# Two graph layers in one kernel: the attention product moved next to z, h turned by eight DMA transposes, x products among the additions, two buffers for h

## The reference

```python
# layer 1, for every sample
q, k = wq @ x, wk @ x                                  # 512 each
att = softmax(leaky_relu(q[None, :] + k[:, None]))     # 512 x 512
x = layernorm(x + relu(adj @ (x @ att.T) + bm))        # h in the kernel
# layer 2, on h (256 rows of 512)
A_l = relu(cosine similarity of the rows of h @ W_lang.T), diagonal 0
A_g = exp(-squared distances of the rows of h @ W_grav.T / (2 sigma^2)), diagonal 0
K   = w * rownorm(A_l * adj) + (1 - w) * rownorm(A_g * adj)
x   = layernorm(h + K @ (h @ W_V.T) @ W_O.T)
```

## Time and profile before

| | us |
|---|---|
| median of 3 runs | 1072.63 (1071.83 to 1072.81) |
| the profiled execution | 1072.26 |
| its span, first to last instruction | 1070.3 |
| TensorE busy | 1043.2 |
| VectorE busy | 877.3 |
| ScalarE busy | 634.3 |
| GpSimd busy | 325.0 |

### The profile page before, as it was taken

One profiled execution on the slowest core, in us unless ns is written; L12 is line 12 of the kernel. 1 busy time (PEld: TensorE's weight loads), 2 busy tenths in 40 slices (PEclk: granted clock), 3 DMA queues, 4 the chain that ended last, 5 costly groups with the idle time before them and its releaser, 6 DMA issues.

```text
span 1070.3 us, 20032 instructions
## 1 busy us (share of the span) xinstructions
PE 1043.2 (97%) x7429; PEld 723.4 (68%) x7429; DVE 877.3 (82%) x2442; ACT 634.3 (59%) x1203; POOL 325.0 (30%) x280
## 2 busy tenths in 40 slices
PE   7989999999999999999999999999999999999995
PEld 5466767677676766767676676767667676766662
DVE  4767787888889888888988888898888889888767
ACT  2656566485665748566574856657485664748431
POOL 0333315243341524324151432405143240514100
PEclk9999999999999999999999999999999999999998
DMA  7020011030301103030020303002030300202011
GB/s 274 21 77 4 1 64 57 1 119 1 119 1 52 68 1 119 1 119 1 34 87 1 118 2 119 1 26 94 2 118 2 116 5 16 104 2 79 1 40 40
DMA packets 22833, 56.33 MB, mean 53 GB/s; under 512 B 1744, under 2 KB 2256, under 8 KB 20688
## 3 DMA queue, kind: packets, MB, share of 16 engines
q1 hardware_dynamic: 22736, 55.06, 14.1%
HBM read 21.50 MB, written 16.78 MB: 36 GB/s over the span
## 4 chain that ended last, share of the span: by engine, by line
PE 92%; issue 3%; DVE 3%; ACT 1%; POOL 1%; DMA 0%; POOLq 0%; DVEq 0%
PE bank L223 26%; PE bank L224 26%; PE bank L225 26%; PE bank L345 3%; PE bank L428 2%; PE bank L479 2%; PE bank L230 2%; PE bank L259 2%; PE bank L419 1%; PE bank L276 0%; DVE h L1057 0%; POOL y L1129 0%; DMA agg_t<-in_wl 0%; DVE y_stat L1022 0%; ACT y L627 0%
## 5 line engine op out<-in xcount | busy, mean ns | idle before, releaser
L1112 POOL TENSOR_TENSOR att_lo<-att,att_hi 128x512 f16<-128x512 f32 x128 | 157.9, 1245 | 219.8 <-ACT att_hi L532 219.8
L862 DVE SCALAR_TENSOR_TENSOR att<-a_row,u_col,vb 128x512 f32<-128x512 f32 x128 | 126.7, 1010 | 30.3 <-POOL att_lo L1112 30.3
L573 ACT ACTIVATE z_hi<-bank 128x512 f16<-128x512 f32 x128 | 75.7, 591 | 117.1 <-PE bank L225 116.4
L223 PE MATMUL bank<-xw_hi,att_hi 128*128 128x257 f16 x512 | 140.5, 274 | 1.2 <-DVE wvo_lo L746 1.0
L225 PE MATMUL bank<-ht_hi,z_lo 128*128 128x256 f16 x512 | 139.6, 273 | 0.0
L223 PE MATMUL bank<-ht_hi,z_hi 128*128 128x256 f16 x512 | 139.6, 273 | 0.0
L224 PE MATMUL bank<-ht_lo,z_hi 128*128 128x256 f16 x512 | 139.6, 273 | 0.0
L225 PE MATMUL bank<-xw_hi,att_lo 128*128 128x257 f16 x512 | 139.5, 272 | 0.0
L224 PE MATMUL bank<-xw_lo,att_hi 128*128 128x257 f16 x512 | 139.1, 272 | 0.0
L869 DVE TENSOR_TENSOR z_lo<-bank,z_hi 128x512 f16<-128x512 f32 x128 | 87.6, 690 | 39.8 <-ACT z_hi L573 37.7
L634 ACT ACTIVATE xw_hi<-bank 128x256 f16<-128x256 f32 x128 | 49.1, 385 | 107.4 <-PE bank L225 107.4
(11 more groups left out here) (173 smaller groups left out, 2703.4 us busy)
## 6 DMA issues: line engine op xcount, KB each, us to landing
x_in<-in_x SPq DMA_DIRECT2D x16, 1024.0 KB, 5.5
x_res<-x_in SPq DMA_DIRECT2D x16, 1024.0 KB, 5.3
out_y<-o SPq DMA_DIRECT2D x32, 512.0 KB, 3.3
agg_t<-in_wl SPq DMA_DIRECT2D x4, 256.0 KB, 3.6
y<-in_wg SPq DMA_DIRECT2D x1, 1024.0 KB, 9.3
o<-in_wv SPq DMA_DIRECT2D x1, 1024.0 KB, 11.5
h<-in_woT SPq DMA_DIRECT2D x1, 1024.0 KB, 13.7
att<-in_adjT SPq DMA_DIRECT2D x1, 256.0 KB, 4.1
```

Source lines behind the costliest of these rows:

```text
L223: pe.matmul(dst, ah, bh, start=(i == 0 and first), stop=False, skip_group_check=skip)
L573: act.activation(z_hi[:, g, :], bank[g % 4][:], ACT.Copy).then_inc(s["z_hi_done"], 1)
L862: dve.scalar_tensor_tensor(out=att[:, g % 2, :], in0=a_row[:, j, :], scalar=u_col[:, j, n:n + 1], in1=vb[:, g % 2, :], op0=ALU.mult, op1=A ...
L1112: pool.tensor_tensor(att_lo[:, n[0], n[1], :], att[:, g % 2, :], att_hi[:, n[0], n[1], :], ALU.subtract).then_inc(s["att_lo_done"], 1)
```

## The change

The arithmetic of every tile stays. What changes is the place of the work, who does some of it, and where the tiles lie.

- h, ht_hi and ht_lo get two buffers, by the pair's parity. To make room v_hi, v_lo become parts of z_hi, z_lo, kt becomes a part of t, diag_junk a part of vb.
- h of pair q is split before it is turned: h_hi by ScalarE, h_lo by GpSimd, in fp16, in the space of att_hi, att_lo. Eight DMA transposes of 128 x 512 on SP's queue then write ht_hi and ht_lo. Only pair 0 is still turned by TensorE.
- The attention products stand right behind the z products, the turn of agg behind them, ahead of t. On ScalarE and VectorE the attention tiles are interleaved with z_hi and z_lo from the start of the step.
- `k_rows`, `t_rows` and the exps for the attention of pair r are at the end of step p, not in step p + 1. For pair 1 they stand in step 0 on TensorE, and at the end of step -1's list on VectorE and ScalarE.
- The x products, in banks 0 to 2, stand between the t products and the additions. The v products follow the additions.
- The scaling of a_l by s_l is done by ScalarE (`k_scale`).
- o_stats, o_norm and the store of pair p - 1 come in step p as before, but all the o_stats of the last pair follow all its residuals.

Lines of the diff, cut to the core:

```diff
-        h = sb("h", [2 * OC, N])
-        ht_hi, ht_lo = sb("ht_hi", [DC, 2 * O], F16), sb("ht_lo", [DC, 2 * O], F16)
+        h2 = sb("h", [2, 2 * OC, N])
+        ht2_hi, ht2_lo = sb("ht_hi", [2, DC, 2 * O], F16), sb("ht_lo", [2, DC, 2 * O], F16)
...
+        v_hi, v_lo = z_hi[:, 0:2 * OC, :], z_lo[:, 0:2 * OC, :]
+        diag_junk = vb[:].rearrange("p a (b n) -> p (a b) n", n=P)
...
+        kt_hi, kt_lo = t_hi[:, 0:2], t_lo[:, 0:2]
+        h_hi, h_lo = att_hi[:, 0], att_lo[:, 0]
...
+            def turn_h(pair):
+
+                hi, lo = ht_of(pair)
+                for k in range(4):
+                    cols = slice(k * P, (k + 1) * P)
+                    sp.wait_ge(s["h_hi_done"], 4 * (pair - 1) + k + 1)
+                    sp.dma_start_transpose(hi[:, :, cols], h_hi[:, k, :]).then_inc(s["ht_hi_landed"], 16)
+                    sp.wait_ge(s["h_lo_done"], 4 * (pair - 1) + k + 1)
+                    sp.dma_start_transpose(lo[:, :, cols], h_lo[:, k, :]).then_inc(s["ht_lo_landed"], 16)
...
+                if p >= 1:
+                    store(p - 1)
+                if p >= 0 and l0:
+                    turn_h(q)
```

TensorE's new step (p from 0 on; the products themselves are as before):

```diff
+                if p > 0:
+                    pe.wait_ge(s["ht_hi_landed"], 64 * p)
+                    pe.wait_ge(s["ht_lo_landed"], 64 * p)
+                for g in range(8):
...
+                    if p > 0 and l0 and g == 2:
+                        pe.wait_ge(s["t_done"], 2 * q + 2)
+                    if p > 0 and g < 2:
+                        pe.wait_ge(s["o_done"], 4 * p - 3 + g)
+                    if g >= 4:
+                        pe.wait_ge(s["z_lo_done"], 8 * p + g - 3)
...
+                    if at(p, 0) and g == 1:
+                        k_rows(1)
+
+                if l0:
+                    for k in range(8):
+                        pe.wait_ge(s["att_lo_done"], 8 * q + 4 * (k // NC) + 4)
+                        if k < 4:
+                            pe.wait_ge(s["z_lo_done"], 8 * p + 5 + k)
+                        att_product(q, k)
...
+                if l0:
+                    turn_agg(q)
+                for k in range(4):
+                    t_product(k)
+                if new:
+                    for k in range(3):
                         wx_product(k)
...
+                add_transposed(0)
+                add_transposed(1)
+                norm_rows()
+                if new:
+                    for k in range(3, 6):
                         wx_product(k)
+                else:
+                    v_product(0)
+                add_transposed(2)
+                if new:
+                    wx_product(6)
+                    wx_product(7)
+                add_transposed(3)
+                if new:
+                    v_product(0)
+                v_product(1)
+                v_product(2)
+                turn_k(0)
+                turn_k(1)
+                if new:
+                    pe.wait_ge(s["v_lo_done"], 4 * p + 1)
+                    k_rows(r)
+                v_product(3)
+                for k in range(4):
+                    o_product(k)
```

ScalarE's new step:

```diff
                 if l0:
+                    vb_tile(q, 0)
+                    vb_tile(q, 1)
+                    z_hi_tile(0)
+                    for g in range(8):
+                        att_hi_tile(q, g)
+                        if g < 6:
+                            vb_tile(q, g + 2)
+                        for i, after in enumerate((0, 2, 3, 4, 5, 6)):
+                            if g == after:
+                                z_hi_tile(i + 1)
+                    z_hi_tile(7)
                     for k in range(8):
...
+                        agg_tile(q, k)
+                        if new and k in (1, 3):
+                            x_hi_tile(k // 2)
+                    for k in range(4):
+                        relu_tile(q, k)
...
+                t_hi_tile(0)
+                t_hi_tile(1)
                 if l0:
...
+                    h_hi_tile(0)
+                    h_hi_tile(1)
+                t_hi_tile(2)
                 if l0:
...
+                    h_hi_tile(2)
+                    h_hi_tile(3)
+                t_hi_tile(3)
+                if new:
+                    for k in range(3):
+                        xw_hi_tile(p, k)
```

It goes on with xw_hi 3 to 5, the exps of A_g with xw_hi 6 and 7 between them, v_hi 0, the scaling of a_l, v_hi 1 and 2, kt_hi, v_hi 3, the exps of the attention rows of r. VectorE's new step:

```diff
                 if l0:
...
+                    for g in range(8):
+                        att_tile(q, g)
+                        for i, after in enumerate((0, 1, 3, 4, 5, 6, 7)):
+                            if g == after:
+                                z_lo_tile(i)
+                    z_lo_tile(7)
+                    den(q, 0)
+                    o_stats()
+                    den(q, 1)
+                    den(q, 2)
+                    den(q, 3)
+                    o_norms()
                     for k in range(4, 8):
...
+                        den(q, k)
+                    for k in (0, 2):
+                        y_add_tile(q, k)
+                        y_stat_tile(q, k)
+                    y_stat_tile(q, 1)
+                    y_stat_tile(q, 3)
+                    y_mean(q)
+                    sq_tile(0)
+                    t_lo_tile(0)
+                    sq_tile(1)
+                    sq_bound()
+                    h_tile(q, 0)
+                    h_tile(q, 1)
+                    t_lo_tile(1)
+                    neg_g_tile(0)
+                    h_tile(q, 2)
+                    h_tile(q, 3)
...
+                neg_g_tile(1)
+                t_lo_tile(2)
...
+                if new:
+                    for k in range(3):
+                        xw_lo_tile(p, k)
+                t_lo_tile(3)
+                masked_rows()
+                if new:
+                    for k in range(3, 6):
+                        xw_lo_tile(p, k)
```

More of the change, by code:

```diff
@@ new lines, in k_rows, with att_product @@
+            def k_rows(q):
+                pe.wait_ge(s["q_part_done"], q + 1)
+                for j in range(2):
+                    last = spread(bank[6][:, j * P:(j + 1) * P], q_part[:, j:j + 1])
+                last.then_inc(s["q_mm"], 1)
+                for j, b in enumerate(k_bank(q)):
+                    for n in range(NC):
+                        last = spread(bank[b][:, n * P:(n + 1) * P], qk[:, j * NC + n, 1:2])
+                    last.then_inc(s["k_mm"], 1)
+            def att_product(q, k):
+                j, m = k // NC, slice((k % NC) * P, (k % NC + 1) * P)
+                if k >= 4:
+                    pe.wait_ge(s["agg_done"], 8 * q + k - 3)
+                product(bank[k % 4][:, 0:O + 1], [(att_hi[:, j, n, m], att_lo[:, j, n, m],
+                                                   xw_hi[:, j, n, 0:O + 1], xw_lo[:, j, n, 0:O + 1])
+                                                  for n in range(NC)]).then_inc(s["ot_mm"], 1)
@@ new lines, in turn_agg, with wx_matmuls @@
+            def turn_agg(q):
+                for k in range(4):
+                    if k < 3:
+                        pe.wait_ge(s["agg_done"], 8 * q + (5, 6, 8)[k])
+                    j, c = k // 2, slice((k % 2) * P, (k % 2 + 1) * P)
+                    for m in range(NC):
+                        last = pe.transpose(bank[k][:, m * P:(m + 1) * P], agg_t[:, j, m, c], ident[:])
+                    last.then_inc(s["to_mm"], 1)
+            def wx_matmuls(p, k):
+                j, n = k // NC, slice((k % NC) * P, (k % NC + 1) * P)
+                product(wx_bank(p, k)[:, 0:OW],
+                        [(x_hi[:, j, c, n], x_lo[:, j, c, n], wm_hi[:, c, :], wm_lo[:, c, :])
+                         for c in range(CC)]).then_inc(s["wx_mm"], 1)
@@ L644, in step, with k_scale @@
-                if new and not at(p, -1):
-                    for k in range(4, 8):
-                        xw_hi_tile(k)
+                    act.activation(v_hi[:, k, :], bank[v_bank[k]][:], ACT.Copy).then_inc(s["v_hi_done"], 1)
+                def k_scale():
+                    act.wait_ge(s["sl_done"], p + 1)
+                    for k in range(4):
+                        act.activation(a_l[:, k // 2, k % 2, :], a_l[:, k // 2, k % 2, :], ACT.Copy,
+                                       scale=s_l[:, k:k + 1]).then_inc(s["kl_done"], 1)
@@ L648, in _ @@
+                v_hi_tile(3)
+                if new:
+                    ab_rows(r)
+                    uv_columns(r)
             split_setup0()
@@ new lines, in y_stat_tile, with y_mean @@
+            def y_stat_tile(q, k):
+                if k % 2:
+                    dve.wait_ge(s["y_odd_done"], 2 * q + k // 2 + 1)
+                else:
+                    dve.wait_ge(s["y_done"], 2 * q + k // 2 + 1)
+                dve.bn_stats(y_stat[:, k, :], y[:, k, :]).then_inc(s["y_stat_done"], 1)
+            def y_mean(q):
+                wait(dve, s["y_rstd_done"], q)
+                dve.wait_ge(s["y_stat_done"], 4 * q + 4)
+                dve.tensor_scalar(turn_y[:], y_stat[:, 3, 0:1], 1.0, None, ALU.mult)
+                for k in range(4):
```

(34 more changed lines are left out.)

937 lines of the change are left out of this document (440 added, 497 removed).

## The result

The changed kernel takes 1138.64 us (median of 4 runs, 1137.20 to 1140.08) beside 1072.34 for the kernel before (1071.83 to 1072.81): ratio 1.0618, 95% interval 1.0600 to 1.0637. It is 66 us slower, where 1067.8 was forecast, and lies outside the range of 1056 to 1098.

What follows compares the result with a forecast made beforehand. TensorE's gapless matmul stream was taken as the bound: 13 middle steps of 62.25 us (61.05 + 1.2) in place of 62.80 give -7.2 us, the ends +2.3, so 1067.8 us; range 1056 to 1098.

Steps and rivals of the forecast that it cites:

- the second rival: Ahead of den4, o_norm and x_lo take turns; turn of agg 3.9 us later, 1118.5 us; chance 0.12.
- The sum: Whole run: middle steps -7.2 us and the end steps +2.3 make -4.9 us, assuming VectorE keeps going beside x_lo.
- S: TensorE's stall per middle step from the new order: between 0.8 and 3.3 us, taken as 1.2.
- The low end for S: Middle step with hardly any att held up by att_lo: stall 0.8 us; 1.2 was taken, near this end.
- the first rival: First 25 us of a step: VectorE's chain becomes the bound; 1084.7 us, at the high end 1095; chance 0.24.
- the high end: Middle step where every att that meets att_lo waits for its end: stall 3.3 us.
- The ideal step: Middle step without stalls: 62.80 us less 1.75 of transposes of h on TensorE, 61.05 us.
- att's mean passes 1.3: Sign in the profile after: a mean att duration above 1.3 us would show the forecast wrong.
- I am wrong if: Three signs: TensorE gapless in the middle steps, att's mean above 1.3 us, or no gap in step 0.
- Step 14: Transposes, rows for k and the wait for h gone, 1.0 of stalls added: -4.1 us.
- step 15 and tail: Last step: TensorE ends 1.7 us earlier, but the last four o_stats follow all residuals: 0.1 us.
- Step 0: Pair 1's rows spread there and late z_lo hold up z4 to z6, less the transposes: +6.4 us.

Runs made afterwards that it cites:

- experiment 1: Changed kernel with one added wait: GpSimd starts x_lo only when both halves of o_norm are done; 1092.58 us, ratio 1.0186.
- experiment 10: Changed kernel with only x_lo altered: eight pieces of 128x256 on GpSimd in place of two of 128x1024; 1091.59 us, ratio 1.0167.
- experiment 9: The kernel of experiment 6 with the fifth x remainder, xw_lo4, also ahead of the masked rows; 1055.52 us, ratio 0.9845.
- experiment 3: Changed kernel with every DMA transpose issued twice, the extra one into a spare tile ahead of the real one; 1141.45 us in one run.
- experiment 6: experiment 1 plus statistics in free gaps, xw_lo0 to xw_lo3 earlier, and step 0's k rows and first z_hi, z_lo earlier; 1064.12 us, ratio 0.9922.
- experiment 4: experiment 1 with VectorE's four o_stat tiles moved from behind den0 to ahead of att2, att4, att6 and att7; 1089.70 us, ratio 1.0159.
- experiment 7: Changed kernel with statistics in free attention gaps and xw_lo0 to xw_lo3 earlier, but without GpSimd's wait for the normalisation; 1083.43 us, ratio 1.0102.

## Why the prediction was wrong

**The step that failed** is the one sentence of the second rival, "If VectorE keeps going, x_lo waits and little is lost. The sum takes the latter." VectorE does not keep going: between two of its back-to-back tiles the waiting GpSimd instruction gets its turn, each time. The duration by line after, the 46 us of experiment 1 and the scaling with the size of the piece in experiment 10 show it. The rival got its chance of 0.12 for a choice between two ends that no row read from before decided. The row nearest in kind, sq_lc beside att_lo, pointed to the side that came true, and the sum should have followed it. The trace of before held more: sq_lc at 104.90 us falls on two att_lo tiles in a row and ends at 105.28, 0.03 us behind the end of the first, and the other fourteen held ones lie alike. There the waiting engine got its turn at the edge between two tiles of the other. The Trainium skill ("SBUF — State Buffer", Who interferes with whom) says that, with VectorE in its two-port mode, whichever of the two issues first blocks the other fully; the 2360 ns tile agrees, as the prediction had worked out.

**The rival itself was too small.** It gave S = 5.1 and 1118.5 us; measured S is 67.6 - 61.05 = 6.5. In the step at 553 us the excess is 6.76: 0.59 of waiting for agg in the attention products and 0.6 of smaller delays of z and attention, 2.73 ahead of the turn of agg, 1.3 + 0.36 for the turn and t, nearly all of it the lower clock, and 1.2 around xw_lo. The rival's 3.9 us for two x_lo was near the mark for o_norm (5.54 - 1.91 = 3.6). The lower clock after the gap was in no term; it is 1.5 us in each of ten steps, 15 us, a good fifth of the loss. Two comparisons show it: three steps of the same trace have the same gap without the fall and are shorter by that much, and no middle step of experiments 1 and 10, where the gap is gone or 0.2 us, shows the lower level.

**The low end for S was the wrong end, too.** With the meeting removed (experiment 1) a step is 63.97 us, S = 2.9, inside "between 0.8 and 3.3" but far from the 1.2 taken; 1092.6 us is the first rival's ground (1084.7 to 1095). So even without the meeting the forecast would have had the wrong sign: experiment 1 is 20 us above the kernel before. Its reason failed: "because the median att is 750 ns and only 46 of 128 att waited". The step has three held tiles of eight, att2, att4 and att6, with 1.66 us each, 48 of 128 in all. A median does not see three of eight; it is 743 ns in the changed kernel. The 46 of 128 were already three of eight, and the mean of 1010 ns beside the median of 750 said so too. The hand schedule of the high end came near: in experiment 1 z_lo7 ends 17.2 us after z0 (17.4 in the text), attention product 5 waits 0.6 (1.0 with what was lost before), the two places of xw_lo wait 1.5 (1.7); only the turn of agg is not late at all (0.6).

**What held.** The ideal step: 61.05 against the 61.39 of experiment 9, so the transposes taken from TensorE are worth nearly what was said. The 62.80 of the earlier trace rows that it starts from is the longest of the fourteen steps 0 to 13 of before; the others take 62.67 to 62.71, which puts the ideal at 60.92 and every S above by 0.13 higher. The DMA transposes cost nothing: in the middle step they stood on SP's queue from 592.5 to 603.8 us, landed after 2.5 us, and z0 at 621.2 had 16 us to spare; experiment 3 confirms it. The profile's marks for the rival (o_norm above 1 us a tile, den4 behind x_lo) were the ones that appeared; the mark "att's mean passes 1.3" did not (1079 ns), and was no good as a test. Nor did the two others under "I am wrong if" appear: all three signs watched TensorE's gaps and att, and none the meeting. Step 14 was -3.5 (-4.1 forecast), step 15 and tail -0.7 (0.1).

**Smaller misses.** Step 0 was +9.3 against +6.4, and experiment 6 shows that its z_lo waits cover the attention's own chain, which the prediction did not carry to its end. "Setup is unchanged" missed 2.1 us in the pair of traces. A wait of 0.8 us for agg at the turn of agg in the setup is gone from it, and the new turn needs only five tiles of agg to begin; for the rest no cause is shown, since kernels with the same setup take 76.7 to 78.6 us for it from trace to trace.

**Left open:** why the attention products take 10.9 us in experiment 9 and 10.6 before, which is most of what its middle step has above the ideal (the z products have 0.17 more, 0.12 of it a wait for z_lo); and why the clock fell behind ten of the thirteen like gaps and not behind the other three.

## What to carry to other kernels

Before moving a block of VectorE to where GpSimd works, lay the two engines' timelines over each other: where long GpSimd tiles meet a row of short VectorE tiles, each VectorE tile may wait for a whole GpSimd tile, and a wait on GpSimd (46 us here), a smaller GpSimd tile (47 us here) or work that VectorE puts into time it would wait anyway (a statistic ahead of a held tile, free) gives much of it back. In a schedule laid out by hand, take durations for the very position of a tile, not the median of its line. Order the work of the engine behind TensorE by when TensorE needs each tile: one wait and three reorderings of a few lines turned a change that was 6.2% slower into one 1.5% faster.

## What was not expected of the hardware

- The turns are exact: four VectorE tiles of 0.55 us beside two GpSimd tiles of 2.1 us take 5.54 us, in two kernels alike, and beside pieces of 0.67 us 2.98. Very small VectorE instructions pay the same: neg_gs, two columns, has a median of 222 ns and a maximum of 1125 beside h_lo. The statistic o_stat is not held: none of its 64 tiles in experiment 4 takes more than 0.69 us, though 56 of them stand beside att_lo.
- A gap of 2.7 us ahead of 16 transposes was followed by a lowered clock in ten steps (0.57 over 3.5 us in the one shown) and by 1.00 in three; the wait of 1.0 us in experiment 7 was followed by 1.00.
- Eight DMA transposes of a 128 x 512 fp16 tile each held the queue 1.2 to 1.3 us (one 2.0), 11.3 us together, and landed 2.5 us after issue. The Trainium skill ("VectorE: DVE Perf Modes", The three transpose paths) gives 1309 ns for one 128 x 128 block; four of them would be 5.2 us, an estimate from that page. In the traces four blocks in one DMA land after 2.5 us, half of that, and they decide; how long one block alone takes no run here shows.
